# A counting sort on TensorE: counting before looking up, and destinations in one product of 200 columns

## The reference

```
seg = dst * r + etype
sums = segment_sum(x[src], seg, n * r)
cnt = segment_sum(1, seg, n * r)
h = (sums / max(cnt, 1)).reshape(n, r, -1)
out = einsum('nrf,rfo->no', h, W) + x @ root + bias
```

## Time and profile before

| what | us |
|---|---|
| median of 3 runs (lowest, highest) | 4822.65 (4818.04, 4827.08) |
| the profiled execution's own time | 4810.64 |
| its span | 4808.9 |
| busy over the span: PE, its weight loads, DVE, ACT, POOL | 3834.3, 2952.3, 3239.0, 1714.3, 2386.6 |

### The profile page before, as it was taken

How to read it: one execution, slowest core, us unless ns; L and a number is a source line. 1 busy time by engine, 2 the same in 40 slices (tenths; PEclk the granted TensorE clock), 3 DMA queues, 4 the chain that set the end, 5 groups by cost and what they waited for, 6 DMA issues and landing times.

```text
span 4808.9 us, 111129 instructions
## 1 busy us (share of the span) xinstructions
PE 3834.3 (80%) x27568; PEld 2952.3 (61%) x27569; DVE 3239.0 (67%) x8054; ACT 1714.3 (36%) x4185; POOL 2386.6 (50%) x2369
## 2 busy tenths in 40 slices
PE   3589888889966666666678888998888998888997
PEld 2556655566645445555546667775667776666776
DVE  8858777777877777777745555665555765555666
ACT  0025555555511111111132224773222774222575
POOL 2877777777047777777700004770001773000675
PEclk9559898989987887788869999999999999999999
DMA  1111111111033232333317886774887773888676
GB/s 43 37 46 54 49 48 50 49 48 38 1 85 77 76 78 76 78 78 77 71 11 202 229 229 202 208 209 123 230 232 214 207 209 115 232 229 230 192 209 179
DMA packets 791567, 607.25 MB, mean 126 GB/s; under 512 B 172939, under 2 KB 703933, under 8 KB 791510
## 3 DMA queue, kind: packets, MB, share of 16 engines
q1 hardware_dynamic: 679798, 329.11, 24.7%
q0 software_dynamic: 111712, 277.47, 20.4%
HBM read 361.22 MB, written 245.08 MB: 126 GB/s over the span
## 4 chain that ended last, share of the span: by engine, by line
PE 41%; POOL 23%; issue 17%; DMA 7%; DVE 7%; SPq 1%; DVEq 1%; ACT 1%; POOLq 0%; ACTq 0%
PE ps L825 21%; PE ps L822 18%; POOL slot_rows L631 11%; POOL y_sb L642 10%; DMA mid<-msgs,block_idx 3%; POOL mid L654 3%; DMA iota_h<-codes 2%; DVE mid L1606 1%; DMA a_code<-codes 1%; DMA y_sb<-in_x_dram,idx_st 1%; DVE mid L1542 1%; SPq L571 1%; DVE y_sb L1274 1%; DVE mid L1622 0%; PE ps L913 0%
## 5 line engine op out<-in xcount | busy, mean ns | idle before, releaser
L654 POOL DMA_INDIRECT mid<-msgs,block_idx x750 | 715.4, 954 | 1654.2 <-DMA msgs<-mid 1408.0
L822 PE MATMUL ps<-mid 128*128 128x128 f32 (+3 forms) x7668 | 1234.2, 299 | 89.3 <-DMA mid<-msgs,block_idx 34.9
L666 ACT ACTIVATE mid<-ps 13x512 f16<-13x512 f16 (+3 forms) x1665 | 638.6, 399 | 1369.2 <-PE ps L825 900.7
L825 PE MATMUL ps<-y_sb,mid 128*128 x6552 | 943.5, 287 | 221.7 <-issue 137.3
L822 PEld LDWEIGHTS ps<-mid 128*128 128x128 f32 (+3 forms) x7668 | 857.7, 175 | 317.8 <-issue 263.4
L825 PEld LDWEIGHTS ps<-y_sb,mid 128*128 128x128 f32 x6552 | 792.7, 191 | 374.4 <-issue 374.2
L642 POOL DMA_INDIRECT y_sb<-in_x_dram,idx_st x808 | 790.7, 979 | 417.9 <-issue 250.3
L631 POOL DMA_INDIRECT slot_rows<-y_sb,row_st x784 | 862.9, 1101 | 265.6 <-issue 237.2
L1622 DVE TENSOR_SCALAR mid<-iota,slot_lo,slot_w 128x128 f32<-128x128 f32 x2250 | 664.1, 378 | 314.2 <-PE ps L822 302.4
L825 PE MATMUL ps<-y_sb 128*128 128x193 f32 x1616 | 434.3, 423 | 270.7 <-DVE mid L1542 186.5
L825 PEld LDWEIGHTS ps<-mid 100*128 100x128 f32 (+2 forms) x1884 | 349.9, 207 | 385.0 <-ACT mid L666 211.6
(11 more groups left out here) (246 smaller groups left out, 3357.6 us busy)
## 6 DMA issues: line engine op xcount, KB each, us to landing
msgs<-mid SPq DMA_DIRECT2D x819, 256.0 KB, 3.6
y_sb<-slot_rows SPq DMA_DIRECT2D x101, 268.0 KB, 3.2
a_code<-codes SPq DMA_DIRECT2D x411, 64.0 KB, 3.6
iota_h<-codes SPq DMA_DIRECT2D x408, 64.0 KB, 3.6
y_sb<-in_edge_attr_dram SPq DMA_DIRECT2D x54, 256.0 KB
y_sb<-in_x_dram,idx_st POOLq DMA_INDIRECT x808, 2.5
slot_rows<-y_sb,row_st POOLq DMA_INDIRECT x784
mid<-msgs,block_idx POOLq DMA_INDIRECT x750, 3.7
```

What stands on the lines that cost most here:

```text
L654: nc.gpsimd.indirect_dma_start(out=rows[:, s % RB, :], out_offset=None, in_=msg_blocks, in_offset=bass.IndirectOffsetOnAxis(ap=block_idx[: ...
L666: return nc.scalar.activation(o, i, func, **kw)
L822: return nc.tensor.matmul(o, a, b, start=False, stop=False, skip_group_check=True)
L825: return nc.tensor.matmul(o, a, b, start=True, stop=True, skip_group_check=True)
```

## The change

The count of a column is issued ahead of its lookup. ACT's copy of the table for the next column waits for the count as before, and newly also for the lookup that last read its buffer (`table_read`). The lookup still reads the copy that was made before the count. For the destinations `pick_d` is only 128 wide, and next to each `pick_q` lies a second mask, `pick_q` times whether the type is odd (`odd_h`, made once ahead of the sort). One product with 200 moving columns counts all edges in the first 100 and those of odd types in the second; the even ones come by subtraction behind the sort.

```diff
--- before.py
+++ after.py
@@ -191,15 +191,19 @@
         key_bits = words(y_sb, 0, COLS * KEYBITS // 2, F16).rearrange("p (c b) -> p c b", b=KEYBITS)
         at = SORT_AT
         assert COLS * KEYBITS // 2 <= SORT_AT
-        pick_q = [words(y_sb, at + par * GC * Q // 2, GC * Q // 2, F16).rearrange("p (c q t) -> p c q t", q=Q, t=2)
-                  for par in range(2)]
-        at += GC * Q
+
+        pick_qo = [words(y_sb, at + par * GC * Q, GC * Q, F16).rearrange("p (c o q t) -> p c o q t", o=2, q=Q, t=2)
+                   for par in range(2)]
+        pick_q = [t[:, :, 0, :, :] for t in pick_qo]
+        at += 2 * GC * Q
         pick_f = [words(y_sb, at + par * GC * F1 // 2, GC * F1 // 2, F16).rearrange("p (c f t) -> p c f t", f=F1, t=2)
                   for par in range(2)]
         at += GC * F1
-        pick_d = [words(y_sb, at + par * GC * P, GC * P, F16).rearrange("p (c d t) -> p c d t", d=2 * P, t=2)
+        pick_d = [words(y_sb, at + par * GC * P // 2, GC * P // 2, F16).rearrange("p (c d t) -> p c d t", d=P, t=2)
                   for par in range(2)]
-        at += 2 * GC * P
+        at += GC * P
+        odd_h = words(y_sb, COLS * KEYBITS // 2, COLS // 2, F16)
+        assert COLS * KEYBITS // 2 + COLS // 2 <= SORT_AT
         bits_st = words(y_sb, at, GC * KEYBITS, F16).rearrange("p (b c k) -> p b c k", b=2, k=KEYBITS)
         at += GC * KEYBITS
         more_hi = [words(y_sb, at + b * HI // 2, HI // 2, BF16) for b in range(4)]
@@ -350,7 +354,7 @@
                  "rows_summed sums_made tiles_made starts_made cells_made edge_made a_started a_counted b_started "
                  "b_counted cell_picked cell_added diff_made prefix_made table_set masks_made "
                  "qf_picked d_picked turned_q bits_copied q_copied paired same_made looked_up "
-                 "column_counted table_copied mult_made columns_used lo_picked hi_picked perm_used "
+                 "column_counted table_read table_copied mult_made columns_used lo_picked hi_picked perm_used "
                  "sort_done slots_made slots_used idx_made "
                  "sel_made pair_made tile_added s_picked s_turned s_copied s_used s_looked s_taken b_weighted w_step "
                  "a_coded codes_turned codes_made codes_stored pos_step bias_made nodes_cleared chunk_begun n_staged n_turned n_copied n_made "
@@ -687,6 +691,7 @@
 
             def copy_table(c, q):
                 act.wait_ge(S["column_counted"], c + 1)
+                wait_used(act, S["table_read"], c - 1)
                 copy(table[:, q % 2, :], ps[0:Q, 2, 0:F]).then_inc(S["table_copied"], 1)
 
             def copy_bits(n, q):
@@ -929,13 +934,13 @@
                     pe.wait_ge(S["q_copied"], n + 1)
                     wait_used(pe, S["mult_made"], n - 1)
                 pe.wait_ge(S["table_copied"], 4 * n + (i + 1))
-                whole(LOOKED[q][:, i, 0:F], pick_qT[:, q, P * i:P * (i + 1)], table[:, i % 2, :])
+
                 add(ps[0:Q, 2, 0:F], column(pick_q[par], c0 + i), column(pick_f[par], c0 + i)[:, 0:F]
                     ).then_inc(S["column_counted"], 1)
-                for odd in range(2):
-                    m = add(ps[:, 3, P * odd:P * odd + Q], column(pick_d[par], c0 + i)[:, P * odd:P * (odd + 1)],
-                            column(pick_q[par], c0 + i))
-                return m
+                looked = whole(LOOKED[q][:, i, 0:F], pick_qT[:, q, P * i:P * (i + 1)], table[:, i % 2, :])
+                looked.then_inc(S["table_read"], 1)
+                return add(ps[:, 3, 0:2 * Q].rearrange("p (o q) -> p o q", o=2), column(pick_d[par], c0 + i),
+                           pick_qo[par][:, (c0 + i) // 2, :, :, (c0 + i) % 2])
 
             def permute(c, par, ci):
                 pe.wait_ge(S["hi_picked"], c + 1)
@@ -1257,8 +1262,9 @@
 
             in_turns(dve, GROUPS, pick_hist)
 
+            then(v.tensor_copy(odd_h, key2[:, :]))
             bits(key[:, :], raw[:, 1, :], P - 1, ALU.bitwise_and)
-            then(v.scalar_tensor_tensor(d_h[:, :], key2[:, :], float(P), key[:, :], ALU.mult, ALU.add))
+            then(v.tensor_copy(d_h[:, :], key[:, :]))
 
             bits(key2[:, :], raw[:, 0, :], P - 1, ALU.bitwise_and)
             then(v.tensor_scalar(key2[:, :], key2[:, :], float(LOWEST), None, ALU.add))
@@ -1387,8 +1393,12 @@
 
             def pick_dst(g, par, half):
                 at = half * GC // 2
-                m = pick_of(pick_d[par][:, at // 2:at // 2 + GC // 4, :, :],
-                            in_pairs(d_h[:, ds(g * GC + at, GC // 2)]), 2 * P)
+                pairs = slice(at // 2, at // 2 + GC // 4)
+                pick_of(pick_d[par][:, pairs, :, :], in_pairs(d_h[:, ds(g * GC + at, GC // 2)]), P)
+                dve.wait_ge(S["qf_picked"], g + 1)
+                m = v.tensor_tensor(pick_qo[par][:, pairs, 1, :, :], pick_qo[par][:, pairs, 0, :, :],
+                                    in_pairs(odd_h[:, ds(g * GC + at, GC // 2)]).unsqueeze(2).to_broadcast(
+                                        [P, GC // 4, Q, 2]), ALU.mult)
                 if half:
                     m.then_inc(S["d_picked"], 1)
 
@@ -1466,8 +1476,9 @@
             then(v.tensor_scalar(code, slot_j, float(1 - LOWEST), 0.0, ALU.add, ALU.max))
             then(v.tensor_scalar(slot_used, code, 0.0, None, ALU.is_gt))
             inv = inv_cnt[:, :].rearrange("p (q o) -> p q o", o=2)
-            for odd in range(2):
-                then(v.tensor_scalar(inv[:, :, odd], ps[:, 3, P * odd:P * odd + Q], 1.0, None, ALU.max))
+            then(v.tensor_copy(inv[:, :, 1], ps[:, 3, Q:2 * Q]))
+            then(v.tensor_tensor(inv[:, :, 0], ps[:, 3, 0:Q], inv[:, :, 1], ALU.subtract))
+            then(v.tensor_scalar(inv_cnt[:, :], inv_cnt[:, :], 1.0, None, ALU.max))
             then(v.reciprocal(inv_cnt[:, :], inv_cnt[:, :]))
             then(v.tensor_copy(inv_parts[:, :, 0], inv_cnt))
             then(v.tensor_tensor(inv_rest, inv_cnt, inv_parts[:, :, 0], ALU.subtract))
```

## The result

The changed kernel takes 4830.68 us (median of 20 runs, 4822.94 to 4840.83), the kernel before, run beside it, 4817.56 (20 runs, 4809.1 to 4828.01). The ratio is 1.0028, with a 95% interval from 1.0022 to 1.0035: **slower by 13 us**. That is inside the range, 5 us above the time that was forecast, and just past the 0.2% that was to count as no change.

A forecast was written before the change was run, and what follows sets the result against it. Scatters were taken to pace the sort to about 1141 us, then PE to 1336; +7.9 - 1.7 - 3 + 0.2 = +3.4 us on the median 4822.65 gave 4826 us, range 4807 to 4844.

The forecast's parts named there:

- What bounds the kernel: Sort: scatters set the pace up to about 1141 us, PE from there to 1336 us.
- 1, PE per column: PE's stretch after 1141 us: both f32 lookup loads come behind a short count, 0.35 us a column; +7.9 us.
- 2, groups 0 and 1: First two groups, half clock: lookup leaves the chain, some 9 us go, nearly all hidden; -1.7 us.
- 3, DVE: Mask of 2048 becomes a mask and a multiplication, 0.68 + 0.57 us, beside PE's work; cost 0.
- 4, the scatters' waits: Scatters up to 1141 us: shorter DVE masks save some waits, mostly waited again at the next mask; -3 us.
- 5, the small ones: One operation more before the sort, covered; one behind it, +0.2 us; table copies' extra semaphore wait, 0.
- Scatters freed by 16 us: Rival, middle of sort: shorter masks' full -16 us comes, giving 4813; both faster rivals together had chance 0.22.
- Load saved is 0.1 us saved: Rival, PE's stretch: the removed load saves 18 us over 176 columns, giving 4800; both faster rivals together 0.22.
- Scatters wait longer: Rival, middle of sort: longer batches shift masks so more scatters are caught, +11 us, 4840; 0.32 with weaker forms past +9.6.
- Nothing happens: Rival, whole kernel: nothing is bound by what the change shortens and no costs come, 4822; 0.46 together with the forecast.

The follow-up runs named there:

- e6: Kernel before with ACT's builds spread: two chunks a group in the first 16 groups, then three in two groups; 4732.42 us.
- e11: Kernel of e4 with builds spread evenly, five in three groups, and ACT's groups written out without a loop; 4701.74 us.
- e1: Kernel before with only the count put ahead of the lookup; two destination products and the wide mask stay; 4838.60 us.
- e2: Changed kernel with the lookup first again and without `table_read`, keeping the joined product and short masks; 4814.06 us.
- e4: Changed kernel with each lookup issued one column later, behind the next column's permutation of 500 columns; 4805.77 us.
- e5: Kernel before with one more product of 128 columns per column, its result not kept; 4835.43 us.
- e3: Changed kernel with the lookup moved behind the joined destination product: count, destinations, lookup; 4816.13 us.

## Why the prediction was right, and where it was not

*What bounds the kernel: right.* The scatters pace the sort to the last awaited build and PE from there. e6 to e11 say the same from the other side, since with the builds spread the gathers begin 66 to 112 us earlier than in the kernel with the same order on PE.

*1, PE per column: right in mechanism and size.* Here the forecast's 0.35 us was worked out from the spacing of the loads in the earlier trace rows, 0.36 measured; +7.9 us were taken for PE's stretch, +9.2 measured (203 us was its forecast length, 203.1 it is). Two steps inside the 0.35 were each 0.06 off, in opposite directions: the load of the destinations starts 0.16 us after the first f32 load and not 0.22, its product 0.11 behind that and not 0.05. That the f32 loads do it is shown by e1 (the same 0.36 without the joined product), e2 (4.33 us with it) and e4 (0.28 once they stand behind the permutation). The Trainium skill (TensorE: Matmul & The Clock Gate, LDWEIGHTS) gives columns / 1.2 ns for a load, which is 107 ns for 128 columns. Beside the 0.11 us between the f32 loads in the earlier trace rows that agrees. Taken as a saving for each load left out it does not hold here: e2, with one f16 load fewer a column, shortens a batch of four columns by 0.01 us.

*2, groups 0 and 1: right in its effect, -2.3 us for -1.7.* No scatter waits for rows near 366 us any more. That both groups would be shorter by 4 us was too much: from the first sum of positions to the second it went from 23.1 to 21.2 us. The 0.3 us were taken for all 32 columns, but only every second column had waited for its table: in the change a lookup starts 0.68 or 0.83 us after the one before it (344.98 to 345.66, 347.63 to 348.46) in place of 1.0 within such a pair, and from pair to pair nothing is gained.

*3, DVE: right.* Two parts of 0.679 and 0.573 us; nobody waits for them.

*4, the scatters' waits: **the step that failed**.* "I take -3" was measured as +6.5. The step took the gain of the shorter masks, cut down to a part, as its middle. That gain is real (7 us less at the destination masks) and, as the step itself argued, mostly waited again elsewhere (-2.0 in e2). But it took the waits at the other masks as unchanged, and the shift of all masks against the scatters, named in the same step and carried as a rival with +11, was the larger term: +12.0 in e1, +7.6 in e5 with one more product a column and nothing else, and in the change itself 19 us more at the `pick_hi` masks. The rival is right in kind, at about half of its size, though not by longer batches alone (e3 and e4). The mean scatter went to 1.080, in the band of 1.05 to 1.09 that was to confirm the forecast, which was too wide to tell -3 from +6.5: over 484 scatters 0.01 us is 5 us.

*5, the small ones: right.* From the last sum to the gathers +0.3 us, +0.2 forecast.

*The sum.* Forecast +7.9 - 1.7 - 3 + 0.2 = +3.4; measured at the gathers 9.2 - 2.3 + 6.5 + 0.3 = +13.7. The time came out only 5 us over the forecast of 4826, because the first three runs of the kernel before had their median 5 us above that of the twenty beside which the change was measured: against those twenty the forecast difference of +3.4 was 10 us short. That the time itself came so near is luck. The outcome, a change past +9.6, had a chance of 0.32.

*The rivals.* Scatters freed by 16 us: not so, 2 us in e2's trace. Load saved is 0.1 us saved: refuted by e2. Scatters wait longer: right in kind. Nothing happens: true of the joined product alone (e2), refuted by e1's 21 us for the order.

## What to carry to other kernels

Before moving a product, look at what its weight load hides behind: against a place behind a product of 500 columns, two f32 loads cost 0.01 us more behind one of 200 (e3) and 0.08 more behind one of 50, and taking away a cheap f16 load doesn't pay that back. Where an engine's instructions block another engine's, a change of spacing on a third engine is a term of its own, with its own sign, and a band that is to confirm a small term must be as narrow as that term times its count. And ask first what makes the stage wait: here the place of ACT's builds, with its loop written out, was worth 117 us, the order of PE's products 10 to 30.

## What the runs showed of the hardware that was not expected

- A loop on ACT with a body of 8 groups stood idle 1.95 us at its way back. PE paused for 2.39 us, and from 0.7 us after the pause its granted clock was 0.50 (1.2 GHz) for some 7 us: a group of 23 us in place of 17.35. Written out, without a loop, the kernel had no such regular groups. That it is the fetching of the loop's code is not shown.
- The scatters, whose own work is the same in all kernels, changed their mean from 1.065 (e2) to 1.071, 1.073, 1.075, 1.080, 1.084 and 1.090 us (e1) with the place and length of DVE's masks. The Trainium skill (SBUF — State Buffer, Who interferes with whom) gives the lock behind it; the earlier trace rows agree with 1.56 us for a scatter caught in a mask. That batches 0.13 us longer, with the same masks, cost 7.6 us in 70 chunks (e5) is in no row of before.
- A wait absorbed part of an added product: 0.05 us a column more on PE left the batch of four columns 0.13 us longer, not 0.2, because lookups that waited for their table no longer did.
